# Attention values held in the scores' banks, a state product of small tiles, a ring of four banks, and another order in the opening

## The reference

```python
qkv = layernorm(x) @ W_attn + b_attn
q, k, v = split(qkv)                       # 16 heads of 32
q, k = elu(q) + 1, elu(k) + 1
# for each head, token by token:
kv   = kv + k[:, None] * v[None, :]
ksum = ksum + k
y    = (q @ kv) / (q . ksum + 1e-6)
x = x + y @ W_proj + b_proj
# feed-forward: both operands clipped and rounded to fp8 (e4m3), then multiplied in fp16
x = x + fp8(layernorm(x)) @ fp8(W_ffn).T + b_ffn
```

## Time and profile before

| | us |
|---|---|
| median of 3 runs | 1105.98 (1104.98 to 1107.2) |
| the profiled execution | 1102.66 |
| its span, which all views below cover | 1100.8 |
| PE, DVE, POOL, ACT busy | 1025.5, 827.4, 718.8, 568.9 |
| start of the scores of chunks 0, 1, 2, 3 | 61.68, 81.06, 103.24, 119.81 |
| eight chunks (12 to 19) from scores to scores | 130.34 |

### The profile page before, as it was taken

One profiled execution on the slowest core, in us unless ns is written; L12 is line 12 of the kernel. 1 busy time (PEld: TensorE's weight loads), 2 busy tenths in 40 slices (PEclk: granted clock), 3 DMA queues, 4 the chain that ended last, 5 costly groups with the idle time before them and its releaser, 6 DMA issues.

```text
span 1100.8 us, 25183 instructions
## 1 busy us (share of the span) xinstructions
PE 1025.5 (93%) x10112; PEld 557.2 (51%) x10112; DVE 827.4 (75%) x1447; ACT 568.9 (52%) x937; POOL 718.8 (65%) x718
## 2 busy tenths in 40 slices
PE   5877999999999999999999999999999999999976
PEld 2334555555555555555554555555455555555543
DVE  7888767777786867878686786777778777775655
ACT  4454463654646456364555546465554745546343
POOL 5346788576677757667576767758666775864444
PEclk9989999999999999999999999999999999999999
DMA  9201312213131231312213141221313123130011
GB/s 315 39 11 29 78 39 64 59 48 74 42 71 49 59 68 35 87 41 58 63 40 78 45 78 43 60 68 41 73 49 69 43 66 61 40 63 26 25 30 58
DMA packets 121924, 65.59 MB, mean 60 GB/s; under 512 B 102480, under 2 KB 102480, under 8 KB 121808
## 3 DMA queue, kind: packets, MB, share of 16 engines
q1 hardware_dynamic: 121808, 63.99, 23.4%
HBM read 22.81 MB, written 16.78 MB: 36 GB/s over the span
## 4 chain that ended last, share of the span: by engine, by line
PE 41%; POOL 30%; DVE 16%; ACT 6%; issue 6%; DMA 1%; SPq 0%; POOLq 0%; DVEq 0%; ACTq 0%
PE R L219 32%; POOL sm L948 9%; POOL st L916 6%; PE Y L219 5%; POOL xs L964 5%; POOL xn L918 4%; POOL xs L933 4%; DVE st L605 3%; POOL x L918 3%; DVE xs L717 3%; ACT rel L446 2%; PE S L311 2%; ACT qkv L443 2%; DVE state L700 1%; DVE cum L650 1%
## 5 line engine op out<-in xcount | busy, mean ns | idle before, releaser
L219 PE MATMUL R<-xt,wh 128*128 128x512 f16 x960 | 288.1, 382 | 18.2 <-ACT rel L446 17.7
L628 DVE SCALAR_TENSOR_TENSOR qkv<-qkv,rel 128x512 f32<-128x512 f32 x128 | 119.5, 934 | 133.7 <-ACT rel L446 131.9
L916 POOL TENSOR_TENSOR st<-st,half 128x1 f32<-128x1 f32 x128 | 93.4, 730 | 149.1 <-DVE st L610 143.2
L948 POOL TENSOR_SCALAR_AFFINE_SELECT sm<-sm 128x512 f32<-128x512 f32 x184 | 183.4, 1024 | 7.3 <-ACT sm L431 7.3
L219 PE MATMUL R<-xt,wl 128*128 128x512 f16 x480 | 183.0, 381 | 0.0
L219 PEld LDWEIGHTS R<-xt,wh 128*128 128x128 f16 x960 | 89.3, 98 | 124.1 <-ACT rel L446 21.3
L219 PE MATMUL R<-wh,xt 128*128 128x512 f16 x480 | 150.3, 379 | 0.0
L943 POOL TENSOR_TENSOR cum<-cum,qkv 128x512 f32<-128x512 f32 x64 | 84.8, 1325 | 97.6 <-DVE cum L648 50.4
L955 POOL TENSOR_TENSOR yl<-y,yh 128x512 f16<-128x512 f32 x64 | 74.8, 1169 | 97.1 <-ACT yh L431 96.2
L443 ACT ACTIVATE qkv<-R,bqk,wm 128x512 f32<-128x512 f32 x128 | 99.2, 775 | 63.9 <-PE R L219 63.3
L431 ACT ACTIVATE yh<-y 128x512 f16<-128x512 f32 x64 | 40.3, 630 | 155.7 <-DVE y L710 155.7
(11 more groups left out here) (108 smaller groups left out, 1878.8 us busy)
## 6 DMA issues: line engine op xcount, KB each, us to landing
xs<-in_L_attn_x SPq DMA_DIRECT2D x64, 256.0 KB, 2.9
out<-xs SPq DMA_DIRECT2D x64, 256.0 KB, 2.0
qkv<-in_L_attn_W_attn SPq DMA_DIRECT2D x3, 1024.0 KB, 7.9
xs<-in_L_attn_W_proj SPq DMA_DIRECT2D x1, 1024.0 KB, 8.9
rden<-in_L_ffn_weight SPq DMA_DIRECT2D x1, 1024.0 KB, 12.4
x2t<-x2b SPq DMA_TRANSPOSE x62, 2.4
xt<-xnhl SPq DMA_TRANSPOSE x60, 3.2
bv<-in_L_attn_b_attn SPq DMA_DIRECT2D x1, 256.0 KB, 8.1
```

What stands on the lines that cost most here:

```text
L219: return e.matmul(out, a, b, start=start, stop=stop, skip_group_check=True)
L628: e.scalar_tensor_tensor(qkv[j % 2][:, i, :], qkv[j % 2][:, i, :], 1.0, rel[:, (u - 1) % 2, :], ALU.min, ALU.add).then_inc(s_phi, 1)
L916: e.tensor_tensor(row[:, 10:11], row[:, 9:10], half[:, :], ALU.pow).then_inc(s_rs, 1)
L948: e.affine_select(out=four(sm[:, h, :]), in_=four(sm[:, h, :]), compare_op=ALU.is_ge, fill=0.0, base=0, pattern=[[0, 4], [1, P]], channel_ ...
```

## The change

In the middle: Y becomes the first 128 columns of each of the four S banks, one bank for a head h, with group g on the rows 32g. Its former bank joins the ring, which has four members, and the key transposes are taken from the ring. The state is kept as one 128x128 matrix (head h on the rows 32h, group g in the columns 32g), the state product is sixteen matmuls of 32 rows and 32 weight columns, and the state update on DVE one instruction. The masked product runs head by head, and within a head group by group. `scores(n)` waits for y of the chunk before, and `values(n)` for the copies of all four heads' scores. W_proj is loaded in the matching order of rows, in four transfers. POOL adds b_proj behind the masks. The negated mean is no longer made on DVE; POOL subtracts the mean.

In the opening: the sizes of the q, k and projection weights are sums of absolute values, made on ACT (the power-of-two scale below them is a factor 2 smaller); the size of v stays a maximum on DVE. The third and fourth `most` stand behind the groups 4 and 10, the scans of block 0 among the feature groups, the lent matmuls of chunk 0 behind the third group of chunk 0, `parts_less` (a small reduction of constants made on POOL) ahead of the first scale, `ffn_low` behind y of chunk 0 and `ffn_high` behind y of chunk 1. The parts of W_ffn use other buffers.

```diff
@@ build: ring, banks, sizes
-NR = 3
+NR = 4
...
-        state = sb("state", [P, 2, D], F32)
+        state = sb("state", [P, 2, P], F32)
...
-        S = [psum(f"S{i}") for i in range(4)]
-        Y = psum("Y")
+        S = ctx.enter_context(nc.psum_tensor("S", [P, 4, D], F32))
+
+        Y = S[:, :, 0:P]
@@ TensorE: the key transposes take a bank of the ring
             def k_tokens(n):
...
-                if n >= 2:
-                    pe.wait_ge(s_y, n - 1)
+                out = take(("ktok", n), s_ktok, state_count(n))
                 for g in range(4):
                     pe.wait_ge(s_phi, phi_count(j, 4 + g))
-                transposes(Y, [src[:, 4 + g, cols] for g in range(4)]).then_inc(s_ktr, 1)
+                transposes(out, [src[:, 4 + g, cols] for g in range(4)]).then_inc(s_ktr, 1)
@@ TensorE: scores wait for the values before them
             def scores(n):
                 src, j, c, cols = parts(n)
+                if n:
+                    pe.wait_ge(s_y, n)
...
-                        if n and g == 0:
-                            if h < dve_heads(n - 1):
-                                pe.wait_ge(s_smd, masked_dve(n - 1, h))
-                            else:
-                                pe.wait_ge(s_scopy, masked_act(n - 1, h))
-                        mm = e.matmul(S[h][:, g * P:(g + 1) * P], src[rows, 4 + g, cols], src[rows, g, cols],
+                        mm = e.matmul(S[:, h, g * P:(g + 1) * P], src[rows, 4 + g, cols], src[rows, g, cols],
@@ TensorE: values
             def values(n):
+
                 src, j, c, cols = parts(n)
                 first = n % PER == 0
-                if n:
-                    pe.wait_ge(s_y, n)
-                if n + 1 < NT and (n + 1) % PER != PER - 1:
-                    pe.wait_ge(s_ktok, state_count(n + 1))
+                for h in range(4):
+                    if h < dve_heads(n):
+                        pe.wait_ge(s_smd, masked_dve(n, h))
+                    else:
+                        pe.wait_ge(s_scopy, masked_act(n, h))
                 if not first:
                     pe.wait_ge(s_state, state_count(n - 1))
                     for g in range(4):
-                        matmul(Y[:, g * P:(g + 1) * P], state[:, n % 2, g * P:(g + 1) * P], src[:, g, cols],
-                               g == 0, False)
+                        for h in range(4):
+                            rows = slice(32 * h, 32 * h + 32)
+                            matmul(Y[32 * g:32 * g + 32, h, :], state[rows, n % 2, 32 * g:32 * g + 32],
+                                   src[rows, g, cols], True, False)
                 pe.wait_ge(s_v, n + 1)
-                for g in range(4):
-                    for h in range(4):
-                        if h < dve_heads(n):
-                            pe.wait_ge(s_smd, masked_dve(n, h))
-                        else:
-                            pe.wait_ge(s_sel, masked_act(n, h))
+                for h in range(4):
+                    if h >= dve_heads(n):
+                        pe.wait_ge(s_sel, masked_act(n, h))
+                    for g in range(4):
                         col = (4 * g + h) * 32
-                        mm = matmul(Y[32 * h:32 * h + 32, g * P:(g + 1) * P], src[:, 8 + c, col:col + 32],
-                                    sm[:, h, g * P:(g + 1) * P], first and g == 0, True)
+                        mm = matmul(Y[32 * g:32 * g + 32, h, :], src[:, 8 + c, col:col + 32],
+                                    sm[:, h, g * P:(g + 1) * P], first, True)
@@ TensorE: opening, lend_out of chunk 0 later
-            for m in range(3):
+            for m in range(4):
                 t1(m)
             most(0)
-            t1(3)
             for i in range(12):
                 proj_qkv(0, i)
-                if i in (0, 2):
-                    most(1 if i == 0 else 2)
+                if i in (0, 4, 10):
+                    most((0, 4, 10).index(i) + 1)
             k_tokens(0)
             den(0)
-            most(3)
@@ ScalarE: sizes of the weights
+            def attn_size(i):
+
+                cols = slice(i * D, (i + 1) * D)
+                act.wait_ge(s_wa[i], 16)
+                e.activation(wl[:, :, cols].bitcast(BF16), raw[:, :, cols], ACT.Abs,
+                             accum_out=wm[:, 7 * i:7 * i + 1]).then_inc(s_size, 1)
+
+            def proj_size():
+                act.wait_ge(s_wp, 64)
+                e.activation(wpl[:, :, :].bitcast(BF16), raw_p, ACT.Abs, accum_out=wm[:, 21:22]).then_inc(s_size, 1)
@@ VectorE: state update, statistics, loop
-                e.tensor_scalar(row[:, 8:9], row[:, 6:7], -1.0, None, ALU.mult)
...
-                for h in range(4):
-                    rows = slice(32 * h, 32 * h + 32)
...
-                    if n % PER == 0:
-                        a = e.tensor_copy(new, fresh)
-                    else:
-                        a = e.tensor_tensor(new, fresh, old, ALU.add)
-                a.then_inc(s_state, 1)
+                new, old, fresh = state[:, (n + 1) % 2, :], state[:, n % 2, :], bank["delta", n][:, 0:P]
+                if n % PER == 0:
+                    e.tensor_copy(new, fresh).then_inc(s_state, 1)
+                else:
+                    e.tensor_tensor(new, fresh, old, ALU.add).then_inc(s_state, 1)
...
-                    if n == 0:
-                        ffn_low()
...
-                    if n == 0:
-                        ffn_high()
                     values(n)
                     update(n)
+                    if n == 0:
+                        ffn_low()
+                    if n == 1:
+                        ffn_high()
@@ GpSimd: loop
                         ln1(n + 8)
-                        add_bp(n + 8)
                     scores(n)
                     after(j + 1, 3 * c)
+                    if n + 8 < NT:
+                        add_bp(n + 8)
```

More of the change, by code:

```diff
@@ L279, in den, with lend_out @@
                 mm.then_inc(s_den, 1)
[L281 to L284 removed]
+            def lend_out(j, heads):
+                for h in heads:
+                    out = take(("lent", 4 * j + h), s_rden, 4 * j + h + 1)
                     pe.wait_ge(s_lend, 4)
                     pe.wait_ge(s_third, j + 1)
[L287 removed]
+                    matmul(out[:, :], lend[:, h, :], inverse(j)[2], True, True).then_inc(s_lent, 1)
             def k_tokens(n):
@@ L406, in _ @@
                     ahead(j + 1, 3 * c + 1)
-                    if c == 0:
+                    if c == 0 and j:
                         lend_out(j, (0, 1))
```

132 lines of the change are left out of this document (70 added, 62 removed).

## The result

The changed kernel takes 1164.52 us (median of 4 runs, 1163.3 to 1166.88) where the kernel before, on the same chip, takes 1106.09 (4 runs). The ratio is 1.0531, interval 1.0510 to 1.0552: it is slower by 5.3%, where 5.6% faster was forecast.

The account below looks back on a forecast made before the run. PE, busy 93% of the span, was taken as the bound, with waits above 15.17 us a chunk. Savings 10.8 + 0.45 + 48.1 + 1.7 + 0.5 = 61.5 us took 1105.98 to 1044.5 us; range 1034 to 1066.

Parts of the forecast that it names:

- one small instruction goes from each statistics step: Middle part, DVE: dropping it makes DVE lighter; no separate size given, and nothing priced on POOL.
- C: Rival: POOL's masks still come last, half of 3.9 us per eight chunks stays, 14 us, so 1058; chance 0.07.
- State product: Middle part, PE: sixteen tiles take 0.54 us instead of 0.98, bounds 0.49 to 1.16; 3.15 us less per eight chunks.
- POOL's masks: Middle part: head order and bias behind the masks remove all four POOL excesses, 3.9 us per eight chunks.
- Rival A: State product's tiles overlap no more than four or issue too slowly: 1.16 us each, 34 us, so 1079; chance 0.10.
- The ring: Middle part: four banks save 0.35 us per eight chunks; the 2.3 us Relu wait at blocks' first chunks stays.
- The period: Middle part: eight chunks take 122.9 us instead of 130.3, 48.1 us less over chunks 4 to 55.
- the end: From 1046.69 us on: cheaper state products and updates mostly lengthen waits; 0.5 us less.
- y before scores: New wait of scores for the previous chunk's values: cost 0, up to 0.4 us in one chunk of eight.
- B: Rival: DVE becomes the gate, y about 0.5 us late every second chunk, 14 us, so 1058; chance 0.12.
- D: Rival: scores waiting for y close a loop that decides; slower, 1113 us if y is 1.2 us late; chance 0.02.
- The opening: Up to chunk 3's scores, near 109 us instead of 119.81: 10.8 us less, bounds 4 to 14; chunk 3 gives 0.45.

Follow-up runs that it names:

- after_neg_mean: The changed kernel with one edit undone: DVE makes the negated mean again and POOL adds it instead of subtracting the mean; 1039.95 us, ratio 0.9413.
- the second run: Changed kernel with the negated mean, POOL's b_proj addition back ahead of the masks, and PE waiting for all masks before the masked product; 1080.8 us, ratio 0.9773.
- ring_of_three: The changed kernel with the negated mean and a ring of three banks instead of four, key transposes still a member; 1059.58 us, ratio 0.9591.

## Why the prediction was wrong

**The step that failed** is the clause at the end of the part on the values, "one small instruction goes from each statistics step". It is one half of an edit. DVE's half was named as a small gain; POOL's half, the scaling with another pair of operations, was in the diff and in the description of the change, and was never costed, at nothing or otherwise. No bound was given for an operation that no row of before showed on POOL. Its term is 128 x (2.08 - 0.77) = 168 us of work, of which 124.6 reached the end. None of the four rivals held it: C had POOL's masks late, but from DVE's side and for 14 us. The range, 1034 to 1066, was that of the remaining steps alone, and after_neg_mean lies in it at 1039.95: between the profiled spans the rest gains 60.3 us of the 61.5 forecast. That they meet so closely is partly luck, since steps in it were off in both directions, as listed below.

**The bound.** The earlier trace rows showed POOL at 65%. The period shows more: 96.07 of 130.34 us in the earlier trace rows, with 16 scalings in it. At 1.31 us more each these alone are 21 us, so an estimated 117 of a forecast 122.9: little slack for an engine that also waits for DVE and ACT, with both scalings queued ahead of the masks. (With the fast scaling POOL turned out at 90.62 us of the period, so by its busy time alone it would still have fitted in. It is the order on its queue that carries the delay to PE.) A warning could have been read from the rows of before: had the new form taken the 1.58 us of POOL's bias addition, the period would have held 13 us more of POOL's work, and every chunk 1.6 more ahead of its masks.

**The other steps, read in after_neg_mean.**

State product: forecast 0.54 us from start to next, with 0.49 to 1.16 as bounds. In after and in after_neg_mean it is 0.43 (569.82 to 570.25 above), below the lower end. 32 passes in that time are 13.4 ns each, near the pace of the update's passes. The sum was 0.11 too high; how the 0.43 divides between the tiles (0.22 taken) and the changes of shape (0.27 allowed) no run tells. Rival A fell. TensorEngine Tiling (Array Packing), Instruction Overhead, in the Trainium skill gives about 60 cycles of overhead for each matmul. The prediction applied it to the 32 recorded passes, an estimated 0.80 us, and the trace is well below that. Applied to the sixteen f32 matmuls as the program writes them, it is an estimated 0.40 us, which the trace does not contradict, so the run refutes the first reading only.

POOL's masks: forecast 3.9 us per eight chunks, all waits gone. All are gone, and taking both edits back costs 40.9 us over the run, where 6.5 periods at 3.9 are 25. The mechanism was right. The size was that of the waits in the kernel before; the faster state product asks for the masks some 0.5 us earlier, so the old orders would wait longer in the new kernel. Part of the 40.9 is also that the second run asks for the masks earlier than the old order did. How much each gives isn't shown.

The ring: the Relu wait at a block's first chunk stays, as forecast, but at 0.67 us a block instead of 0.98 in the mean and up to 1.3. The fourth bank was forecast at 0.35 us per eight chunks against the old arrangement; that figure was not tested. Against ring_of_three it is worth 19.6 us in all, since with three banks the transposes wait.

The period: forecast 122.9 us, measured 122.37. From chunk 4 to 56 the gain is 51.2 us, forecast 48.1; chunks 56 to 59 give 1.4 (1.7), the end 0.6 (0.5).

y before scores: forecast to cost nothing. In the middle part y ends 12.4 to 15.5 us after the scores' start, at least 1.2 us before the chunk's end, and no wait for it is in the list above. The tightest chunk, forecast with y at 14.2 of 14.3 us, has it at 13.0. Rivals B and D fell. Only the opening has such a wait, 0.52 us ahead of chunk 1's scores.

The opening, the term furthest off of those that were priced: forecast 11.25 us less with chunk 3, measured 7.04. It held up to chunk 2: the scores of chunks 1 and 2 start at 76.19 and 90.43 (forecast 76 and 92), and the stand at 27 us is gone. Then chunk 2's masked product stands 3.75 us for the mask, and chunk 3's scores come at 113.23 instead of 109:

```profile
101.42 0.43 PE L220 MATMUL S<-sm,qkv 128*32 128x128 f32 x8
105.60 1.24 PE L220 MATMUL S<-sm,qkv 128*32 128x128 f32 x16 [3.75 <-POOL sm L965]
107.23 0.66 PE L220 MATMUL S<-sm,qkv 128*32 128x128 f32 x8 [0.39 <-POOL sm L965]
```

This is the delay behind the feed-forward weight that the prediction named, mis-sized: it had the masks at 104.5 and they come at 107.2, and in the 5.8 us from 105.60 on the granted clock is 0.52, nearly all of it at the lower level, 1.2 GHz.

The parts taken back add up to 22.3 + 18.5 + 8.1 = 48.9 us, and the state product by its rows is 0.55 us in seven of eight chunks, some 25 over chunks 4 to 55: 74 in all, where the whole gains 65. (The 19.6 us of ring_of_three are not in this sum, since that arrangement is neither the old nor the new one.) The sum is above the whole, as it would be if each part is worth its price only while the others keep their waits away; but 18.5 is an upper bound, and the state product by itself was not undone in a run, so the overlap is likely and not shown.

## What to carry to other kernels

Price both ends of an edit that drops an operand: the instruction that goes from one engine and the form that another engine's instruction takes in its place. A form that no row of the trace shows gets a bound like any other unknown, and 128 of them on an engine in the loop are measured alone before they go in. When a busy engine grows with no more instructions, compare the mean time of each of its groups between the two traces first; here one group, POOL's scaling, held all of POOL's growth, and undoing its one edit gave back 124.6 us.

## What the runs showed of the hardware

On POOL, scaling a 128x512 f32 block takes 0.77 us as add and multiply, multiply and add, or multiply twice, and 2.09 us with a subtraction in either place (1.92 with constants); one operation alone, addition or subtraction, takes 1.57. GPSIMD Engine Reference, 3.1, in the Trainium skill gives 768 ns as the best case for 512 elements, and the trace agrees for the three quick forms, at 0.77 us; a pair with a subtraction takes 2.7 times that.

Sixteen 32x32 tiles of f32 with 128 columns go at 13.4 ns a recorded pass (two for each matmul), 0.43 us for a product that takes 0.98 us as four tiles of 128x128.
